# Last stage's row statistics moved into the third stage, and its scale arithmetic rewritten

## What is computed

```
def layernorm(x, eps=1e-5):
    return (x - mean(x)) / sqrt(var(x) + eps)
def act_quant(x):                      # per row
    scale = 127 / clip(max(abs(x)), 1e-5)
    return clip(round(x * scale), -128, 127) / scale
def h_bitlinear(x, w):
    return act_quant(fwht(x)) @ weight_quant(w).T
# out = h_bitlinear(silu(h_bitlinear(x, w_gate)) * h_bitlinear(x, w_up), w_down)
```

## Time and profile before

| | |
|---|---|
| median of three runs | 722.65 us (722.41 to 723.34) |
| span of the profiled execution | 719.6 us |
| that execution's own time | not listed apart; its span is 3.05 us below the median |
| PE busy | 654.6 us, 91% of the span |
| DVE busy | 587.3 us, 82% |
| ACT busy | 468.7 us, 65% |
| POOL busy | 392.7 us, 55% |
| mean granted TensorE clock | 0.993 of full speed |

### The profile page before, as it was taken

The page is one execution under the profiler, slowest core; times in us unless marked ns, Lnnn a source line. Parts: engine busy times, 40 slices in busy tenths (PEclk is TensorE's granted clock), DMA queues, the critical chain, the costliest instruction groups (busy, mean ns, idle before and its releaser), DMA issues.

```text
span 719.6 us, 12514 instructions
## 1 busy us (share of the span) xinstructions
PE 654.6 (91%) x4067; PEld 374.6 (52%) x4098; DVE 587.3 (82%) x1358; ACT 468.7 (65%) x949; POOL 392.7 (55%) x291
## 2 busy tenths in 40 slices
PE   1688899999999999997999999887999999999996
PEld 0365566666666676842434444443544545544543
DVE  6889899999998887376676774788999989999875
ACT  3737567766776655367778732566787788778744
POOL 2023122324132313257998951079999999899970
PEclk9999999999999999999999999999999999999999
DMA  9971333324231323629999931434556655665621
GB/s 221 260 239 23 82 97 81 108 84 111 67 111 23 111 66 81 235 53 274 247 298 209 235 66 23 87 70 88 108 103 118 131 102 104 136 126 106 114 60 45
DMA packets 173132, 88.22 MB, mean 123 GB/s; under 512 B 150547, under 2 KB 152595, under 8 KB 172053
## 3 DMA queue, kind: packets, MB, share of 16 engines
q1 hardware_dynamic: 167188, 71.94, 43.7%
q10 hardware_dynamic: 3408, 11.27, 4.8%
q0 software_dynamic: 2480, 4.33, 3.3%
HBM read 51.20 MB, written 4.19 MB: 77 GB/s over the span
## 4 chain that ended last, share of the span: by engine, by line
PE 44%; DVE 26%; ACT 9%; issue 8%; POOL 6%; DMA 5%; SPq 1%; POOLq 0%; DVEq 0%; ACTq 0%
PE ps L1807 10%; PE ps L1661 7%; PE ps L1733 7%; PE ps L1751 6%; DMA arena<-arena 4%; PE ps L1676 4%; DVE X L1095 3%; DVE arena L1185 2%; PE ps L1787 2%; POOL arena L535 2%; POOL arena L536 2%; DVE y_sm L1490 2%; PE ps L1879 2%; ACT arena L862 2%; PE ps L1847 2%
## 5 line engine op out<-in xcount | busy, mean ns | idle before, releaser
L1661 PE MATMUL ps<-arena 128*128 128x256 f16 x1408 | 159.9, 273 | 10.4 <-DVE arena L1185 6.7
L463 POOL TENSOR_TENSOR arena<-arena 128x256 f16<-128x256 f32 x88 | 57.7, 676 | 180.4 <-ACT arena L634 180.0
L1661 PEld LDWEIGHTS ps<-arena 128*128 128x128 f16 x1408 | 135.7, 98 | 35.5 <-DVE arena L1185 10.4
L535 POOL TENSOR_TENSOR arena<-arena 128x1024 f32<-128x1024 f32 x44 | 103.7, 2358 | 43.7 <-DVE arena L1464 39.3
L1807 PE MATMUL ps<-arena 128*128 128x512 bf16 x486 | 116.9, 383 | 10.5 <-ACT arena L833 7.7
L536 POOL TENSOR_TENSOR arena<-arena 128x1024 f32<-128x1024 f32 x44 | 104.0, 2363 | 0.0
L1807 PEld LDWEIGHTS ps<-arena 128*128 128x128 bf16 x512 | 48.1, 98 | 69.0 <-DVE arena L1456 9.9
L1676 PE MATMUL ps<-arena 128*128 128x512 f16 x352 | 80.1, 384 | 3.5 <-POOL arena L463 3.5
L627 ACT ACTIVATE arena<-ps,gs 128x256 f32<-128x256 f32 x88 | 40.7, 466 | 52.5 <-PE ps L1661 52.5
L1879 PE MATMUL ps<-arena 128*128 128x512 bf16 x251 | 59.1, 379 | 2.0 <-ACT arena L906 1.8
L1733 PE MATMUL ps<-arena 128*128 128x512 f16 x256 | 59.7, 387 | 0.0
(11 more groups left out here) (158 smaller groups left out, 1211.2 us busy)
## 6 DMA issues: line engine op xcount, KB each, us to landing
arena<-in_ctx_t SPq DMA_DIRECT2D x7, 1024.0 KB, 6.3
arena<-in_wg_t SPq DMA_DIRECT2D x16, 256.0 KB, 3.8
arena<-in_wu_t SPq DMA_DIRECT2D x16, 256.0 KB, 4.4
arena<-in_wd_t SPq DMA_DIRECT2D x16, 256.0 KB, 4.9
arena<-in_ctx_n SPq DMA_DIRECT2D x4, 1024.0 KB, 9.8
arena<-in_wu_t ACTq DMA_DIRECT2D x4, 1024.0 KB, 6.4
arena<-in_wd_t ACTq DMA_DIRECT2D x4, 1024.0 KB, 6.0
out_x<-X SPq DMA_DIRECT2D x16, 256.0 KB, 2.6
```

Of the source, the lines that this page charges most:

```text
L463: nc.gpsimd.tensor_tensor(hl[:, c, at:at + 2 * P], b_h[n % 4], hh[:, c, at:at + 2 * P], ALU.subtract).then_inc(b_hl_r, 1)
L535: nc.gpsimd.tensor_tensor(b[:, :, 0, :], a[:, :, 0, :], a[:, :, 1, :], ALU.add).then_inc(d_bfp, 1)
L1661: last = M(bank(n % 2)[:, 2 * P * i:2 * P * i + 2 * P], W[:, b, c * P:c * P + P], part[:, b, at:at + 2 * P], start=(b == 0 and part is xhT ...
```

## The change

The statistics of the last block's tiles are taken in the third stage, each one step after the tile is final (`d_stats`, step k for tile k - 3), without the addition of the constant. Tiles 14 and 15 are final only at that stage's end, so theirs stand in step 0 of the last stage, between low parts 0 and 1. Mean and variance of all 16 tiles are kept. The addition, the root on POOL and the shift are done for eight tiles at once, twice (`d_variances`, `d_roots`, `d_shifts`). The front scales take three instructions behind the reduction in place of five: the maximum with the division by 127, the reciprocal, which is ACT's scale, and the two scales of gate and up as one instruction two columns wide. The back scales take four instructions in place of five. A table of weight scales (`wback`) is made once. ACT's rounding of the front waits only for the reciprocal.

```diff
-        room = {"a": "a", "b": "b", "c": "a", "d": "b"}
+        room = {"a": "a", "b": "b", "c": "a"}
+        mv_d, ve_d = sb("mv_d", [P, NT, 2]), sb("ve_d", [P, NT, 1])
+        rstd_d, shift_d = sb("rstd_d", [P, NT, 1]), sb("shift_d", [P, NT, 1])
...
+        D_PARTS = ((0, 8), (8, NT))
...
+            def d_roots(part):
+                first, end = D_PARTS[part]
+                pool.wait_ge(d_var, part + 1)
+                nc.gpsimd.tensor_tensor(rstd_d[:, first:end, 0], ve_d[:, first:end, 0], mhalf[:, :].to_broadcast([P, end - first]),
+                                        ALU.pow).then_inc(d_root, 1)
...
-                elif k < NT - 2:
-                    root("d", k - NT + 4, k % 2)
+                elif k == NT - 4:
+                    d_roots(0)
...
-                if on(k + 2):
-                    root("d", k + 2, u)
+                if at(k, 0):
+                    d_roots(1)
...
             def d_round(j, w):
-                act.wait_ge(d_fsm, 6 * j + 6)
+                act.wait_ge(d_fsm, 4 * j + 3)
...
             def d_silu(k, u, n):
                 i = 4 * k + n
+                if n == 0:
+                    act.wait_ge(d_fsm, 4 * k + 4)
...
-                    act.wait_ge(d_ysm, 7 * j + 7)
+                    act.wait_ge(d_ysm, 6 * j + 6)
...
             def d_normal(j, u):
-                act.wait_ge(d_shift, j - 3)
+                if at(j, 4):
+                    act.wait_ge(d_shift, 1)
+                if at(j, 7):
+                    act.wait_ge(d_shift, 2)
...
-                V.tensor_scalar(nthr[:, :], wscale[:, :], -0.5, None, ALU.mult).then_inc(prep, 1)
+                V.tensor_scalar(wback[:, 0:2], wscale[:, 0:2], ISQ_D, None, ALU.mult).then_inc(prep, 1)
+                V.tensor_scalar(wback[:, 2:3], wscale[:, 2:3], ISQ_I1, None, ALU.mult).then_inc(prep, 1)
...
-                if at(k, NT - 4):
-                    stats("d", 0, 0)
-                if at(k, NT - 3):
-                    stats("d", 1, 1)
...
                 if at(k, NT - 2):
-                    norm("d", 1, 1, d_xn[1], d_xn_r)
-                    stats("d", 2, 0)
+                    d_normalised(1)
                 if on(k - 2):
                     add_readout(k - 2, u)
+                if on(k - 3):
+                    d_stats(k - 3)
+                if at(k, NT - 5):
+                    d_variances(0)
                 if at(k, NT - 2):
                     d_low(0)
                 if at(k, NT - 1):
+                    d_shifts(0)
                     front_scales(0, 0)
-                    stats("d", 3, 1)
...
+            def d_stats(j):
+                u = j % 2
+                wait(dve, d_stat, 2 * j - 2)
+                V.bn_stats(bn["b"][:, u, :], tile_of(X, j)).then_inc(d_stat, 1)
+                dve.wait_ge(d_stat, 2 * j + 1)
+                V.memset(carrier["b"][:, u:u + 1], 0.0)
+                V.bn_aggr(mv_d[:, j, :], bn["b"][:, u, :]).then_inc(d_stat, 1)
+
+            def d_variances(part):
+                first, end = D_PARTS[part]
+                dve.wait_ge(d_stat, 2 * end)
+                V.tensor_scalar(ve_d[:, first:end, 0], mv_d[:, first:end, 1], LN_EPS, None, ALU.add).then_inc(d_var, 1)
+
+            def d_shifts(part):
+                first, end = D_PARTS[part]
+                dve.wait_ge(d_root, part + 1)
+                V.scalar_tensor_tensor(shift_d[:, first:end, 0], mv_d[:, first:end, 0], -1.0, rstd_d[:, first:end, 0],
+                                       ALU.mult, ALU.mult).then_inc(d_shift, 1)
...
             def front_scales(j, u):
-                n = 6 * j
+                n = 4 * j
...
-                V.tensor_scalar(c[1], c[0], ISQ_D, Q_EPS, ALU.mult, ALU.max).then_inc(d_fsm, 1)
+                V.tensor_scalar(c[1], c[0], Q_EPS / ISQ_D, 1.0 / 127.0, ALU.max, ALU.mult).then_inc(d_fsm, 1)
                 dve.wait_ge(d_fsm, n + 2)
-                V.reciprocal(c[2], c[1]).then_inc(d_fsm, 1)
-                V.tensor_scalar(c[4], c[1], 1.0 / 127.0, wscale[:, 0:1], ALU.mult, ALU.mult).then_inc(d_fsm, 1)
-                V.tensor_scalar(c[5], c[1], 1.0 / 127.0, wscale[:, 1:2], ALU.mult, ALU.mult).then_inc(d_fsm, 1)
-                dve.wait_ge(d_fsm, n + 3)
-                V.tensor_scalar(c[3], c[2], 127.0 * ISQ_D, None, ALU.mult).then_inc(d_fsm, 1)
+                V.reciprocal(c[3], c[1]).then_inc(d_fsm, 1)
+                V.tensor_scalar(f_sm[:, u, 4:6], wback[:, 0:2], c[1], None, ALU.mult).then_inc(d_fsm, 1)
...
             def back_scales(j, u):
-                n = 7 * j
+                n = 6 * j
                 dve.wait_ge(d_ysm, n + 2)
-                V.tensor_reduce(c[3], y_sm[:, u, 0:2], AX.X, ALU.max).then_inc(d_ysm, 1)
+                V.tensor_scalar(c[4], c[0], Q_EPS / ISQ_I1, c[1], ALU.max, ALU.max).then_inc(d_ysm, 1)
                 dve.wait_ge(d_ysm, n + 3)
-                V.tensor_scalar(c[4], c[3], ISQ_I1, Q_EPS, ALU.mult, ALU.max).then_inc(d_ysm, 1)
+                V.tensor_scalar(c[5], c[4], 1.0 / 127.0, None, ALU.mult).then_inc(d_ysm, 1)
                 dve.wait_ge(d_ysm, n + 4)
-                V.reciprocal(c[5], c[4]).then_inc(d_ysm, 1)
-                V.tensor_scalar(c[7], c[4], 1.0 / 127.0, wscale[:, 2:3], ALU.mult, ALU.mult).then_inc(d_ysm, 1)
-                dve.wait_ge(d_ysm, n + 5)
-                V.tensor_scalar(c[6], c[5], 127.0 * ISQ_I1, None, ALU.mult).then_inc(d_ysm, 1)
+                V.reciprocal(c[6], c[5]).then_inc(d_ysm, 1)
+                V.tensor_scalar(c[7], c[5], wback[:, 2:3], None, ALU.mult).then_inc(d_ysm, 1)
...
             def d_body(k, u):
-                if ahead:
-                    stats("d", k + 2, u)
+                if at(k, 0):
+                    dve.wait_ge(c_add, NT)
+                    d_stats(NT - 2)
+                    d_stats(NT - 1)
+                    d_variances(1)
                 if whole:
                     d_lo(k, 1)
...
-                if ahead:
-                    d_center(k + 2, u)
+                if at(k, 1):
+                    d_shifts(1)
```

32 lines of the change are left out of this document (17 added, 15 removed).

## The result

The changed kernel takes **726.05 us** (median of 5 executions, 724.05 to 731.58); the kernel before, in the same rounds, 722.41 (722.03 to 723.34). The ratio is 1.0066, 95% interval 1.0035 to 1.0097: slower by a little, clear of the noise. So the change costs between nothing that can be told and 0.7%, where 715.0 was forecast and 712.4 to 718.0 given as the range.

A forecast was written before the change was run, and what follows sets the result against it. A loop over DVE and ACT was taken to bound the last stage's tiles, PE following. Ramp 0.1, steady tiles 7.1, tile 14 0.26 and final chain 0.15 give 7.6 us less: 715.0, range 712.4 to 718.0.

The forecast's parts named there:

- the price of the two-column product: Front scales, last stage: 0.12 us taken for one product two columns wide with a pointer, upper bound 0.20.
- rival (d): Third stage: POOL holds up the moved statistics, cost 3.3 us, 1.25 more in 13 tiles; time 731; chance 0.04.
- The period: Steady tiles 5 to 13 of the last stage: from 15.64 to 14.85 us a tile, 7.1 us in all.
- the back scales: Last stage, per tile: four new instructions take 0.63 us instead of 0.68 for five; 0.08 was given to them.
- the pattern: Tile 14, without statistics, root, shift or normalised tile to prepare, returned its low part after 14.85 us; model for steady tiles.
- The wait of the second low part for ACT: Last stage: DVE's second low part waits for ACT, 0.44 us in tile 14; expected in each of tiles 5 to 13.
- PE's wait for the turned rows: Last stage, tiles 5 to 13: PE's wait for line 833 was to be gone or below 0.2.
- The third stage: Statistics cost 0.93 us a tile under DVE's 2.04 us wait for PE, leaving about 1.1; PE's period unchanged.
- The start of tile 1: Ramp of the last stage: PE's start of tile 1 comes about 1.2 us later.
- The clock drop of step 4: Last stage, tile 4: the dip near 500 us stays, first product 1.24 us longer; tile 4 gains nothing.
- POOL is not the bound: Concerns the rival that POOL becomes the last stage's bound: 15.09 us a tile, time 717.2; chance 0.13.
- (c): Last stage: PE becomes the bound, 14.55 us of work a tile, gain 11.5, time 711.2; chance 0.08.

The follow-up runs named there:

- e1: The changed kernel with its two-column product written as two products of one column, nothing else; 719.76 us.
- e12: The changed kernel with single products, SiLU 0 not waiting for the scales, small matmuls in step 3, statistics of tiles 14 and 15 ending the third stage; 717.76 us.
- e5: The changed kernel with the old front and back scales, so only statistics moved and eight-wide roots; 716.47 to 727.90 us, median 1.6 below the kernel before.
- e8: The changed kernel with the two-column product issued as tensor-with-tensor; product 141 to 143 ns with no POOL stage running, otherwise a wait of 0.90 to 0.99 us.
- e15: The changed kernel, two-column product and SiLU 0's wait included, plus thirteen small matmuls in step 3; 724.59 us.
- e16: The changed kernel itself measured once more, in the same rounds as e15; same median as e15, a loss of 2.5 us.
- e3: The changed kernel with the wait for the gate and up scales moved from ahead of SiLU 0 to ahead of the turned rows; 725.63 us.
- e13: The kernel before with thirteen unused statistics added in the third stage, last stage left alone; 722.43 against 723.03 us.
- e10: The changed kernel with single products and SiLU 0 not waiting for the scales, leaving out the low half of TensorE's hidden-value product; period 15.11 us.
- e11: The changed kernel with single products and SiLU 0 not waiting for the scales, maximum of y over half the columns on VectorE; period 14.53 us.

## Why the prediction was wrong, point by point

**The step that failed** is the price of the two-column product in the front scales: "the whole duration of one with a pointer, 0.20, is its upper bound". It takes 0.93 in the queue of a steady tile, which makes the period 0.60 longer. The bound was taken from rows of one column, and width was treated as a matter of duration only. But the trace of before had a row that spoke: one normalisation of 1378 ns among others of 540, a tensor with scalars from SBUF to SBUF beside a busy POOL. It was used in rival (d), for the statistics, which do not wait (660 to 685 ns, all sixteen), and not asked of the new form that the change brings in. The rival with the right mechanism was given to the wrong instruction. The pair is not the whole miss: e1, without it, still took 719.76 where 718.0 was the upper end of the range.

**The period**, forecast 14.85, was 15.71. The 0.86 divide by the runs into four:

- 0.60 is the pair against two single products (15.71 to 15.11).
- 0.12 is that single products save 0.06 in front, not 0.18 (1.22 us from the reduction to the next stage in e12, 1.28 in the kernel before and in e5).
- 0.06 is the back scales, which were given 0.08 and save 0.02. From the set's first instruction to the rounding it is 0.83 us in a steady tile of e5 (612.35 to 613.18), with the old ones, and 0.81 in e12 (612.03 to 612.84). The rounding waits for the whole set, as the text says, and the new set's last instruction is the dearer one with a pointer.
- 0.08 is the pattern. The same stretch takes 0.85 and 0.75 us in the kernel before, in a steady tile (from 614.82) and in tile 14 (from 661.69); ACT's timeline has the two roundings:

```profile
615.67 1.15 ACT L862 ACTIVATE arena<-arena,y_sm 128x1024 f32<-128x1024 f32 x1 [0.64 <-DVE y_sm L1504]
...
662.44 1.15 ACT L862 ACTIVATE arena<-arena,y_sm 128x1024 f32<-128x1024 f32 x1 [0.63 <-DVE y_sm L1504]
```

In the traces of all kernels the longer figure stands in steps 6 to 13 (but for one of before, 1.09) and the shorter one in steps 3 to 5 and 14 (0.83 to 0.84 against 0.75 to 0.76 in e5, 0.81 to 0.82 against 0.73 to 0.74 in e1). Steps 6 to 13 are just those that `tiles` runs in a loop on DVE and ACT; the others are unrolled. So the pattern was read from an unrolled step and used for looped ones, in eight of the nine tiles. Why a looped step is later no run tests. Up to the third hidden product tile 14 took 10.40 us, and e5, with the statistics moved and the old scales, takes 10.48. 9 x 0.86 = 7.7 us, nearly the whole forecast gain.

**What was right.** The frame: the loop of VectorE and ScalarE, TensorE following, tile 14 as the pattern; the stretch behind the third hidden product is 4.71 us in the forecast, in e5 and in e12. (e12 also has tile 14's 10.40 us up to there, by the accident that its scales save the 0.08 by which the pattern was short.) The wait of the second low part for ACT: 0.52 (0.44 foreseen). PE's wait for the turned rows is gone only in the kernels without the pair; in the changed kernel it is 0.30 to 0.46 us, which the forecast did not have. The third stage: 0.93 under the wait, 1.22 left where 1.1 was foreseen, TensorE's period unchanged at 7.33. The eight roots at once: 1.65 us, none of it waited for. The last chain: about 0.1 against 0.15. The start of tile 1: +1.08 where 1.2 was said, though made of two parts, 0.8 from the statistics and 0.3 from a table load for which there was no term.

**Tile 14 and step 4.** Tile 14 lost 0.52 by the pair instead of gaining 0.26. The clock drop of step 4, forecast to stay, is gone in the profiled executions of the changed kernel, e8, e15 and e16, and there in e3's. That gave 0.4 us back in the trace, but nothing shows it to be the change's doing: e13 has the last stage of before, and its profiled execution has no drop either (step 4 of 15.58 us against 16.09).

**The rivals.** POOL is not the bound (its 0.83 us of waiting are still there, and 0.77 more). (c) looked true by the timeline and fell by e10; its figure of 14.55 was met only in e11, 14.53, with VectorE lighter by 1 us, where TensorE has no gap left. That this is then its bound is argued, not tested. (d) was right in that something is held up by POOL, and wrong in where.

## What to carry to other kernels

Before two small VectorE instructions become one wider one, look at whether GpSimd is busy beside them: one column cost 0.19 to 0.21 us in every one of its cases, two columns up to 2.4. An upper bound taken from nearest rows holds only for what these rows share with the new instruction; when its shape crosses from one element to more, an odd row of the old trace, like the one normalisation that took 1378 ns, is the row to take. And an instruction set off from the end of a chain, such as a scale that nobody needs yet, should not be the one that the next engine's semaphore counts.

## What was unexpected of the hardware

- A product of 128x2 values takes as long as GpSimd's running instruction has left: 209 ns with GpSimd idle, 922 in the median, 2391 at most. GpSimd's root of eight columns is an exception: beside it the pair took 209. The addition of eight columns for the roots behaves alike: 172 ns in step 0, and 762 in the third stage beside a POOL instruction of 1.16.
- With a second wait ahead of the first SiLU, its table load of 1.28 us no longer ran while the engine was idle, but behind the wait for TensorE: at 449.48 instead of 447.26.
- With thirteen matmuls that compute nothing the granted clock was 1.00 where it was 0.50 in the trace without them, and one step 2.5 us shorter. The drop does not come in every execution without them.
- TensorE busy for 14.9 of 15.1 us was not the bound: with 0.9 us less work it waited, and the tile took as long.
